# Graph network, layer 0: edge units dealt anew over the four product blocks, logits made turned, the edge operand's product on DVE

## What is computed

```
msg_s = (s_n @ Ws_src)[src] + (s_n @ Ws_dst)[dst]          # 64 scalars
msg_v = (v_n  . Wv_src)[src] + (v_n  . Wv_dst)[dst]        # 32 vectors
w1    = rbf @ W_rbf                                         # 16 -> 224 edge weights
m1_s, m1_v = _cg_tp(msg_s, msg_v, y0, y1, w1 ...)           # 96 scalars, 128 vectors
a = (m1_s @ W_alpha).reshape(e, 4, 16); a = where(a > 0, a, 0.2 * a)
a = sum(a * alpha_dot)                                      # one logit per head
alpha = softmax of a over the edges of one destination
val_s = m1_s @ Ws_val;  val_v = m1_v . Wv_val
val_v = val_v * sigmoid(val_s @ Wg); val_s = sigmoid(val_s)
m2 = _cg_tp(val_s, val_v, y0, y1, w2 ...); h = m2 @ W_vlin
agg = segment_sum(alpha * h, dst)
```

## Time and profile before

| | |
|---|---|
| device time, median of 3 runs (lowest, highest) | 9950.54 us (9944.16, 9958.43) |
| span of the profiled execution, first to last instruction | 8679.9 us |
| that execution's own device time | not given; the median of the runs lies 1270.6 us above its span |
| mean granted TensorE clock, of full speed | 0.947 |
| PE, DVE, POOL, ACT busy, share of the span | 88%, 84%, 69%, 37% |

### The profile page before, as it was taken

One profiled execution on the slowest core, in us unless ns is written; L12 is line 12 of the kernel. 1 busy time (PEld: TensorE's weight loads), 2 busy tenths in 40 slices (PEclk: granted clock), 3 DMA queues, 4 the chain that ended last, 5 costly groups with the idle time before them and its releaser, 6 DMA issues. The chain is left out here.

```text
span 8679.9 us, 218293 instructions
## 1 busy us (share of the span) xinstructions
PE 7627.6 (88%) x60373; PEld 5771.5 (66%) x60374; DVE 7274.4 (84%) x17597; ACT 3252.4 (37%) x8375; POOL 6016.9 (69%) x5890
## 2 busy tenths in 40 slices
PE   2599999999999999999999999887968888888888
PEld 1487777877877787877787778776644444444445
DVE  4699999999999999999999999775368888888886
ACT  1244444444444444444444444332222222222223
POOL 0477777777777777777777777651037777777774
PEclk9799999999999999999999999987569999999999
DMA  4344444444444444444444444321012222222222
GB/s 53 78 101 99 102 100 101 102 100 101 101 102 101 101 101 99 102 100 100 100 101 102 101 102 100 77 75 29 11 37 67 67 67 67 67 67 67 67 67 61
DMA packets 616622, 725.52 MB, mean 84 GB/s; under 512 B 284132, under 2 KB 390884, under 8 KB 616573
## 3 DMA queue, kind: packets, MB, share of 16 engines
q0 software_dynamic: 225408, 385.00, 20.4%
q1 hardware_dynamic: 391165, 339.92, 15.3%
HBM read 708.40 MB, written 16.06 MB: 83 GB/s over the span
## 5 line engine op out<-in xcount | busy, mean ns | idle before, releaser
L778 PE MATMUL bank_pair<-w_msg,blocks 128*128 128x160 f32 (+2 forms) x15640 | 2078.7, 288 | 126.8 <-DVE blocks L1030 98.2
L720 POOL DMA_INDIRECT got_src<-src_tab,idx x1564 | 1661.5, 1062 | 659.4 <-POOL idx L714 358.5
L778 PEld LDWEIGHTS bank_pair<-w_msg,blocks 128*128 128x128 f32 x15640 | 1972.7, 192 | 218.5 <-DVE blocks L1030 218.5
L1504 POOL DMA_INDIRECT gotf<-f_tab,idx x1568 | 1702.3, 1086 | 514.2 <-issue 477.4
L720 POOL DMA_INDIRECT got_dst<-dst_tab,idx x1564 | 1486.3, 950 | 528.7 <-issue 503.7
L802 PEld LDWEIGHTS bank_pair<-weights_t,product 128*128 128x128 f32 x12896 | 1498.7, 195 | 309.9 <-issue 295.6
L802 PE MATMUL bank_pair<-weights_t,product 128*128 128x128 f32 x12896 | 1575.5, 281 | 9.5 <-ACT weights_t L932 8.2
L1545 PE MATMUL bank_pair<-val,to_node 128*128 128x385 f32 x3136 | 1247.6, 545 | 5.0 <-DVE val L1659 5.0
L1600 ACT ACTIVATE val<-pre,y_edge 128x160 f32<-128x160 f32 x1568 | 542.8, 417 | 1534.0 <-DVE pre L1640 1531.4
L1545 PEld LDWEIGHTS bank_pair<-val,to_node 128*128 128x128 f32 x3136 | 621.6, 208 | 536.8 <-issue 270.1
L767 PE MATMUL bank_pair<-edge,w_edge 64*128 64x512 f32 x3128 | 884.8, 642 | 9.5 <-DVE blocks L1030 9.5
(11 more groups left out here) (268 smaller groups left out, 11950.3 us busy)
## 6 DMA issues: line engine op xcount, KB each, us to landing
rbf<-in_rbf SPq DMA_DIRECT2D x391, 256.0 KB
dst_bc<-in_dst_rows SPq DMA_DIRECT2D x391, 256.0 KB
y<-in_y SPq DMA_DIRECT2D x391, 128.0 KB
y<-in_y SPq DMA_DIRECT2D x391, 96.0 KB
gotf<-f_tab,idx POOLq DMA_INDIRECT x1568, 2.7
got_src<-src_tab,idx POOLq DMA_INDIRECT x1564
got_dst<-dst_tab,idx POOLq DMA_INDIRECT x1564
rbf<-in_rbf SPq DMA_DIRECT2D x392, 32.0 KB, 1.7
```

Source lines behind the costliest of these rows:

```text
L720: pool.indirect_dma_start(out=buf[slot][:, t, :], out_offset=None, in_=table[:, :], in_offset=bass.IndirectOffsetOnAxis(ap=idx[slot][:, c: ...
L778: return nc.tensor.matmul(to, blocks[rows, k, P * t:P * t + P], w_msg[rows, c0:c1], start=start, stop=stop)
L1504: pool.indirect_dma_start(out=got[k][:, t, :], out_offset=None, in_=f_tab[:, :], in_offset=bass.IndirectOffsetOnAxis(ap=idx[k][:, t:t + 1] ...
```

## The change

- The four blocks get other units. `EDGE_SLOTS` and `put_edge` place the harmonics and edge weights anew; each 32-row part of a block now feeds a piece of `w_msg` (LOW_S, HIGH_S, LOW_V, HIGH_V). A tile's messages are four matmuls of 128, 128, 96 and 64 columns in one PSUM tile `message`, where there were five of 160, 160, 128, 96 and 128.
- The attention part is made turned: `add_alpha` holds 64 columns of `w_msg` as weights and streams 256 edges of a block, for two halves of the group and for two blocks: four matmuls whose outputs lie on partitions 0 to 63 and 64 to 127 of `alpha`. TensorE waits for `top` ahead of them.
- `alpha_dot` moves into a matrix `spread` [128, 128]; `spread_logits` is two matmuls of 64 rows and 256 columns on `leaky`. The product with `adot`, the sum per head and ScalarE's wide copy go.
- relu reads `alpha` late in ScalarE's step; the leaky relu is one VectorE instruction of 128x256 at the end of VectorE's step. tanh and `gates` follow the exponentials, and run once all four tiles are done.
- All message matmuls now stand ahead of `turn_weights`; nothing stands between it and `turn_message`.
- `edge <- rbf8 * y8` moves from GpSimd to VectorE: right after `blocks` 3 of group g, for group g+2 (`scale_edge`). GpSimd issues its eight gathers in a row.
- `turn_high` moves from the bank pair 0 to the pair 3. The setup issues 8 small DMAs for `spread` in place of one for `adot`.

```diff
 TensorE
-                def message_scalars(t):
-                    add_piece(scalar_tile(t), 0, slice(0, P), t, 0, True, False)
-                    return add_piece(scalar_tile(t), 2, slice(0, P), t, 3, False, True)
-                def message_vectors(t):
-                    add_piece(vectors[:, t, :], 1, slice(0, P), t, 1, True, False)
-                    add_piece(vectors[:, t, 0:96], 2, slice(0, P), t, 2, False, False)
-                    return add_piece(vectors[:, t, :], 3, slice(0, P), t, 4, False, True)
+                def add_alpha(k, piece, start, stop):
+                    first = MSG_FIRST[piece] + 128
+                    for half in range(2):
+                        last = nc.tensor.matmul(alpha[64 * half:64 * half + 64, :], w_msg[:, first:first + 64],
+                                                blocks[:, k, 256 * half:256 * half + 256], start=start, stop=stop)
+                    return last
+                def message_tile(t):
+                    add_piece(t, 0, LOW_S, MSG_C2, MSG_S + 96, True, False)
+                    add_piece(t, 3, HIGH_S, MSG_C2, MSG_S + 96, False, True)
+                    add_piece(t, 2, HIGH_V, MSG_C0, MSG_C1 + 32, True, False)
+                    return add_piece(t, 1, LOW_V, MSG_V, MSG_C1 + 32, False, True)
                 def spread_logits(slot):
-                    for t in range(TILES):
-                        last = nc.tensor.transpose(turn_low[:, P * t:P * t + P], logits_wide[slot][:, t, :], ident[:])
+                    for half in range(2):
+                        rows = slice(64 * half, 64 * half + 64)
+                        last = nc.tensor.matmul(spread_out[:, half, :], spread[rows, :], leaky[slot][rows, :], start=True, stop=True)
...
                         for t in range(TILES):
-                            last = message_scalars(t)
-                        last.then_inc(s["message_s"], 1)
-                        for t in range(3):
-                            message_vectors(t)
+                            last = message_tile(t)
+                        last.then_inc(s["message"], 1)
+                        if mid:
+                            wait_apart(pe, s["top"], g, s["tick_p"])
+                        add_alpha(0, LOW_S, True, False)
+                        add_alpha(3, HIGH_S, False, True).then_inc(s["alpha"], 1)
                     if mid:
                         pe.wait_ge(s["weights"], g)
                         turn_weights().then_inc(s["weights_turned"], 1)
-                    if now:
-                        message_vectors(3).then_inc(s["message"], 1)
...
 GpSimd
-                        gather(slot, (0, 1))
-                    scale_edge(g + 2, slot, use + 1, False)
-                    if further:
-                        gather(slot, (2, 3))
+                        gather(slot, range(TILES))
...
 VectorE
+                def scale_edge(slot, use):
+                    dve.wait_ge(s[f"edge{slot}"], use * 48 + 48)
+                    dve.tensor_tensor(edge[slot][:], rbf8[slot][:], y8[slot][:], ALU.mult).then_inc(s["scaled"], 1)
                         messages(g, 2)
+                        if not (isinstance(g, int) and g + 2 >= NG):
+                            scale_edge(slot, use + 1)
...
+                        dve.wait_ge(s["relu"], g + 1)
+                        dve.scalar_tensor_tensor(leaky[slot][:], alpha, 0.2, rl[:], ALU.mult, ALU.add).then_inc(s["leaky"], 1)
```

More of the change, by code:

```diff
@@ L184, in _ @@
[L184 to L190, removed]
@@ L192, in _ @@
-                Wa, Ws, Wv = A["W_alpha"], A["Ws_val"], A["Wv_val"]
[L193 to L197, removed]
@@ L198, in _, with put_edge @@
-                put(w_msg[0:32, by_b + 96:by_b + 128], Wv[0:32, :])
-                put(w_msg[96:128, by_d + 96:by_d + 128], Wv[32:64, :])
-                for j in range(3):
-                    r, r1 = slice(32 * j, 32 * j + 32), slice(32 * j + 32, 32 * j + 64)
-                    u, w = 32 * ((j + 2) % 3), 32 * ((j + 1) % 3)
-                    put(w_msg[r1, by_b + u:by_b + u + 32], Wv[96:128, :])
-                    put(w_msg[r, by_cv + 32 * j:by_cv + 32 * j + 32], Wv[64:96, :])
-                    put(w_msg[r, by_d + w:by_d + w + 32], Wv[96:128, :])
+                def put_edge(half, pair, part, harmonic, col):
+                    first = 64 * half + NB * EDGE_SLOTS[half].index(harmonic)
+                    put(w_edge[first:first + NB, pair, 32 * part:32 * part + 32], Wr[:, col:col + 32])
@@ new lines, in put_vector @@
+                def put_vector(piece, part, at, frm):
+                    first = MSG_FIRST[piece] + at
+                    put(w_msg[32 * part:32 * part + 32, first:first + 32], Wv[frm, :])
+                s_low, s_high, dot = slice(0, 32), slice(32, 64), slice(64, 96)
+                own, crossed = slice(64, 96), slice(96, 128)
+                put_scalar(LOW_S, 0, s_low)
+                put_vector(LOW_S, 1, 0, crossed)
+                put_scalar(LOW_S, 2, dot)
+                put_vector(LOW_S, 3, 0, own)
@@ L772, in turn_message @@
                     for t in range(TILES):
-                        last = nc.tensor.transpose(pT[:, 512 * half + P * t:512 * half + P * t + P], msg[slot][:, t, c], ident[:])
+                        last = nc.tensor.transpose((turn_low, turn_high)[half][:, P * t:P * t + P], msg[slot][:, t, c], ident[:])
                     last.then_inc(s["turned"], 1)
-                def add_piece(to, k, rows, t, piece, start, stop):
-                    c0, c1 = MSG_COLS[piece]
-                    return nc.tensor.matmul(to, blocks[rows, k, P * t:P * t + P], w_msg[rows, c0:c1], start=start, stop=stop)
```

187 lines of the change are left out of this document (103 added, 84 removed).

## The result

The changed kernel took **10,595.8 us** (median of four runs, 10,520.4 to 10,657.0) where the kernel before took 9953.9 beside it: **1.064 times as long**, 95% interval 1.061 to 1.067. The prediction said 9954, range 9790 to 10,110. It forecast no change; the kernel is 6% slower, outside the range.

A forecast was written before the change was run, and what follows sets the result against it. GpSimd was taken to pace layer 0, TensorE 0.2 us behind; afterwards TensorE's 7.28 + 1.90 + 1.06 + 3.77 = 14.01 us, with extras 14.08 against 14.08. So 9950.5 + 0 x 365 + 3 = 9954 us, range 9790 to 10,110.

The forecast's parts named there:

- the last one of the sum: Whole kernel: the runs' median stays 1270.6 us above the profiled span, giving 9950.5 + 0 x 365 + 3 = 9954 us.
- `add_alpha` 1.06: TensorE, layer 0: the eight 256-column records take 1.06 us, as the edge pair does.
- Turned weights at W+7.28: TensorE, layer 0: turned weights start 2.5 + 3.72 + 1.06 = 7.28 us after W, the start of the second edge pair.
- ScalarE's copy of the turned weights holds the high half by 0.4 us: TensorE, turned messages: idle 0.4 us between low and high halves until ScalarE's copy ends; first edge pair 1.9 after turned weights.
- 14.01 to 14.08 us a group: Layer 0: TensorE's path sums to 14.01 us, 14.08 with first weight loads and late gathers, against 14.08 now.
- GpSimd is freed and its addition waits: GpSimd, layer 0: loses 1.13 us or more, needs 12.7, no longer paces; addition waits for third edge matmul, starting W+1.3.
- VectorE -0.71 us: VectorE, layer 0: net -1.36 + 0.46 + 1.08 - 0.89 = -0.71 us a group, needing at most 13.4, less than TensorE.
- Setup +3 us: Setup: seven more DMAs on SP's queue, at 0.46 us each, add 3 us.
- (b): TensorE, layer 0: ScalarE's copy costs nothing or `add_alpha` streams; gain 183 us, 9770, or half at 9860; chance 0.22.
- (c): VectorE, layer 0: edge product caught by GpSimd's addition, exponentials end W+8.2; loss 329 us, 10,280; chance 0.12.
- (d): TensorE, layer 0: `add_alpha`'s halves run one after the other; 387 us more, 10,340; chance 0.06.
- (e): Freed GpSimd's place is taken by another engine's unseen wait; either sign, mostly slower; chance 0.08.

The follow-up runs named there:

- d1_after: The changed kernel once more, unchanged; 1.059 times the kernel before.
- d1_before: The kernel before once more, unchanged, traced anew; 0.9996 of the kernel before, span 9942.0 us.
- e5_after_half: The changed kernel without the four gathers of destination rows a group in layer 0; 0.918 of the kernel before.
- e3_half_gathers: The kernel before without the four gathers of destination rows a group in layer 0; 0.913 of the kernel before.
- e2_pause: The kernel before with edge product on VectorE and a useless 512-column GpSimd product between the second and third gather pairs; 1.009 of the kernel before.
- e4_half_paced: e3_half_gathers with a GpSimd product of 384 idle columns in place of each left-out gather; 1.012 of the kernel before.
- e3_after_three: The changed kernel with three useless 160-column GpSimd products, one ahead of each gather pair but the first; 1.053 of the kernel before.
- e3_two_halves: The changed kernel with the edge product back on GpSimd in two halves, after the first and third gather pairs; 1.038 of the kernel before.
- d1_edge_on_dve: The kernel before with only the edge product moved to VectorE and GpSimd's eight gathers in a row; 1.054 of the kernel before.
- e2_early_add: d1_edge_on_dve without the GpSimd addition's wait for the third edge matmul; 1.194 of the kernel before.

## Why the prediction was wrong

**The step that failed** is the last one of the sum: "The runs' median lies 1270.6 us above the profiled span; I keep that distance, and the sum on the span is the sum on the time." The distance was no constant. It was 2.1 us a group in layer 0 (16.2 for 14.1, about 830 us) and the rest in layer 1, made by TensorE signals that come late while gathers run, and the change made it 1.6 us a group larger by packing the gathers: 1.6 x 391, about 630 us, against 604 between the medians of d1_after and d1_before. In the sum the packing stood at nothing. A trace whose span lies 13% under the timed runs did not describe what was timed, and 1270 us without an explanation was the largest unknown in the whole working.

Point by point, against the timeline of e5_after_half, where next to nothing disturbs (9 waits put down to "remote", 20 us; W is 3000.24):

- **Messages at W+2.5**: 2.51. **Message records 3.72**: 3.71. **`add_alpha` 1.06**: 1.02. **Turned weights at W+7.28**: 7.24. Right, each of them.
- **ScalarE's copy of the turned weights holds the high half by 0.4 us**: 0.40, released by `weights_t`. Right; over the stretch TensorE waits there in 266 groups of 281, 0.47 us in the mean. The first edge pair came at W+9.34 for 9.18.
- **14.01 to 14.08 us a group**: 14.17 here, 4000 / 281 = 14.23 in the mean. e3_half_gathers, the kernel before under the same cut, has 4000 / 283 = 14.13. The two ratios, 0.918 and 0.913, put the change at 0.5% slower with the disturbance gone: half a per cent off the forecast of no change. With four gathers GpSimd paces neither of the two, so what freeing it was worth is not in this comparison.
- **GpSimd is freed and its addition waits**: right (it starts at W+1.31 for 1.3 here, and waits 3.7 us a group in the changed kernel). What I called slack that "swallows most late gathers" was also the gap that the product had held open between two sets of four gathers. I priced the gathers "in a row" only by GpSimd's own time.
- **VectorE -0.71 us**: wrong against the kernel as timed. The edge product cost 0.95 for the 1.08 taken, but the 0.89 of the sums was no longer there to be had: 259 ns each in d1_before. Without it the balance is +0.05 us or so (-1.36 + 0.46 + 0.95). Nor did VectorE set the time: e2_pause, with the edge product on it, loses 0.9%.
- **Setup +3 us**: too small to be told here.

The rivals: (b) is refuted, since the wait of 0.4 us stands. (c) did not decide: the product is caught now and then (954 ns for 683), but in the group above the exponentials end at W+7.12, as forecast, ahead of the turned weights at W+7.24. The mechanism itself is real, as e4_half_paced shows at a larger dose. (d) is refuted by 1.02. (e), "another engine's wait that I do not see", comes nearest, but it named no place.

**Where the loss is spent.** TensorE's busy time over the stretch of the earlier trace rows was 3833.32 us for 284 groups (13.5 each). The windows of d1_before and of the changed kernel:

```profile
1000.00:5000.00 4000.00, 3496.32 (x31570) 0.95 0.37 88
```

```profile
1000.00:5000.00 4000.00, 3342.14 (x28512) 0.90 0.31 77
```

The changed kernel's own matmuls at full clock, in e5_after_half:

```profile
1000.00:5000.00 4000.00, 3790.00 (x35915) 1.00 0.28 74
```

That is 3496 / 247 = 14.2 and 3342 / 223 = 15.0 us busy, and 2.0 and 2.9 idle; at full clock it is 3790 / 281 = 13.5. Half of the change's 1.7 us is waiting, the other half is the same matmuls taking longer, for the most part at the lower clock after the waits (0.90 for 0.95 in the mean).

**What stays open.** That the packed gathers make the loss is shown by packing and parting them alone. How they do it inside the chip is not: the starved issue of matmuls and the late signals may have one path in common, but no run separates instruction supply from signals. One regularity is in the traces. In the changed kernel 102 signals of the sum come more than 1.5 us late in the stretch; `held` starts 1.1 to 2.0 us after the end of the last gather in each of these, where the next gather of a row would begin after 0.3. There a late signal comes when the gathers have stopped, which would make a long row dear. But half of the 181 late signals of the turned weights in e3_after_three come within 0.3 us of a gather's end, so the delay is no constant, and no run was made to test the link.

Nor is it shown why one pause of about 1 us in the middle does what three of 0.49 do not. The runs with all loads and gathers fit a rule of the longest run of gathers without such a pause (four: 0.990 to 1.025, six: 1.038, eight: 1.053 to 1.194), which was formed after them and not tested on its own; that the second half of e3_two_halves does not count as a pause, at 0.73 to 0.98 us, is read off its result. Within each class other things matter as well: the earlier loads cost 2.3 points, the earlier start 14. And nothing tells why the first trace of the kernel before had no late signals at all.

## What to carry to other kernels

Before a sum is made on a trace, compare its span with the timed runs. If they differ by more than the effect that you forecast, get a trace that agrees with the time, or treat the difference as an unknown cost that the change may scale. Work that stands between DMAs on their issuing engine may be worth its place even when the engine is the pacer: moving it away packs the DMAs. When such an engine is freed, spread its transfers with the steps that it has to do anyway, and not with a wait on the engine that the transfers slow down.

## What the runs showed of the hardware

- A signal of TensorE came 5.85 us after the record of the matmul that gave it, in a group in which GpSimd issued indirect gathers; with four gathers a group instead of eight nearly all came on time. Two signals of different matmuls come together: in d1_edge_on_dve ScalarE and VectorE, waiting since 2835 and 2836 for the turned weights and the last message matmuls, start 0.07 us apart, 1.76 us after the last gather's end:

```profile
2835.02 0.66 PE L785 MATMUL bank_pair<-ident,weights 128*128 128x128 f32 x4
2835.52 0.83 PE L767 MATMUL bank_pair<-w_msg,blocks 128*128 128x128 f32 x6
2837.94 0.94 POOL L720 DMA_INDIRECT got_dst<-dst_tab,idx  x1 [0.30 <-issue]
2840.64 0.60 ACT L948 ACTIVATE weights_t<-bank_pair 128x512 f32<-128x512 f32 x1 [5.57 <-remote]
2840.71 0.56 DVE L1119 TENSOR_TENSOR vec<-bank_pair,y_edge 128x384 f32<-128x384 f32 x1 [4.37 <-remote]
```

- TensorE's issue itself slowed under gathers in e2_early_add (0.36 us a record, against 0.23 at the same clock of 0.50 once they had ended); that kernel needed 4000 / 186 = 21.5 us a group.
- Two matmuls of 256 columns side by side on half the array each (`add_alpha`, eight records) take 1.02 to 1.08 us. At the 0.118 us that a record of 128 columns takes in the sum (3.77 / 32), eight of 256 one after another would take 1.9: the halves do run side by side.
